# Layer 3's cross attention on turned keys kept in a scratch tensor, two heads at a time on 64 rows

## The reference, cut to what matters

```python
q = layer_norm(x, g_norm) @ Wq                 # 4 x 128 x (16 * 64)
k, v = split(context @ Wkv)                    # 4 x 2048 x (16 * 64) each
k, v = with a null key and value in front of each head's
q = q / |q| * q_scale                          # per head
k = k / |k| * k_scale
attn = softmax(q @ k.T * 8)                    # per head
out = layer_norm((attn @ v) @ Wout, g_out)
```

## Time and profile before

| | us |
|---|---|
| median of 3 runs | 1329.11 (1325.99 to 1330.33) |
| the profiled execution | 1332.39 |
| its span, first to last instruction | 1330.6 |
| TensorE busy | 1129.0 (85%) |
| VectorE busy | 626.6 (47%) |
| ScalarE busy | 425.5 (32%) |
| GpSimd busy | 314.3 (24%) |
| mean granted TensorE clock | 0.894 of full speed |

### The profile page before, as it was taken

How to read it: one execution, slowest core, us unless ns; L and a number is a source line. 1 busy time by engine, 2 the same in 40 slices (tenths; PEclk the granted TensorE clock), 3 DMA queues, 4 the chain that set the end, 5 groups by cost and what they waited for, 6 DMA issues and landing times.

```text
span 1330.6 us, 12990 instructions
## 1 busy us (share of the span) xinstructions
PE 1129.0 (85%) x4750; PEld 648.5 (49%) x4750; DVE 626.6 (47%) x1071; ACT 425.5 (32%) x586; POOL 314.3 (24%) x95
## 2 busy tenths in 40 slices
PE   6996789948799976775877999999999999998558
PEld 4663335727566644452756444454454445444434
DVE  3886762156488863123523434343435344432345
ACT  2663404304265542232116322222222222322011
POOL 0000000000000000000000566546654674565000
PEclk9997799957899986696789999899989998999569
DMA  8100000030000020014000000000000000000100
GB/s 337 79 0 1 0 0 0 1 126 0 1 1 1 1 95 0 0 35 202 1 1 0 16 17 20 16 16 17 20 16 16 16 20 12 20 16 4 69 1 8
DMA packets 21366, 40.15 MB, mean 30 GB/s; under 512 B 2496, under 2 KB 18880, under 8 KB 19648
## 3 DMA queue, kind: packets, MB, share of 16 engines
q1 hardware_dynamic: 21312, 39.41, 8.0%
HBM read 39.14 MB, written 0.26 MB: 30 GB/s over the span
## 4 chain that ended last, share of the span: by engine, by line
PE 77%; DVE 12%; ACT 7%; issue 2%; POOL 1%; DMA 0%; POOLq 0%; DVEq 0%; ACTq 0%
PE PSUM L1918 16%; PE PSUM L1922 16%; PE PSUM L1451 9%; PE PSUM L1512 2%; PE PSUM L1653 2%; PE PSUM L1664 2%; PE PSUM L1483 2%; PE PSUM L1947 1%; PE PSUM L1953 1%; PE PSUM L1460 1%; PE PSUM L2028 1%; DVE ARENA L926 1%; DVE HN L754 1%; PE PSUM L1611 1%; POOL RSTD L366 1%
## 5 line engine op out<-in xcount | busy, mean ns | idle before, releaser
L424 POOL TENSOR_TENSOR ARENA<-ARENA 128x2048 f32<-128x2048 f32 x64 | 288.6, 4510 | 196.5 <-ACT ARENA L684 196.5
L1292 DVE TENSOR_TENSOR ARENA<-PSUM,RK 128x512 f32<-128x512 f32 x256 | 175.6, 691 | 271.7 <-PE PSUM L1918 269.9
L1918 PE MATMUL PSUM<-ARENA,CK 128*128 128x512 f32 x512 | 257.3, 606 | 5.1 <-DVE ARENA L1292 4.3
L1922 PE MATMUL PSUM<-ARENA,CK 128*128 128x512 f32 x512 | 253.4, 598 | 5.8 <-ACT ARENA L706 3.7
L684 ACT ACTIVATE ARENA<-ARENA,CK 128x2048 f32<-128x2048 f32 x64 | 128.1, 2002 | 349.8 <-DVE ARENA L1292 349.8
L1922 PEld LDWEIGHTS PSUM<-ARENA,CK 128*128 128x128 f32 x512 | 97.6, 191 | 131.7 <-issue 113.2
L1918 PEld LDWEIGHTS PSUM<-ARENA,CK 128*128 128x128 f32 x512 | 97.6, 194 | 126.8 <-issue 97.7
L366 POOL TENSOR_TENSOR RSTD<-VE,MHALF 128x4 f32<-128x4 f32 x17 | 17.1, 1008 | 565.3 <-DVE VE L751 565.3
L1451 PE MATMUL PSUM<-WK,CT 128*128 128x512 f32 x256 | 124.1, 607 | 0.0
L454 ACT ACTIVATE SQ<-PSUM 128x512 f32<-128x512 f32 x128 | 76.2, 597 | 67.3 <-PE PSUM L1451 59.5
L773 DVE TENSOR_REDUCE RK<-SQ 128x8 f32<-128x512 f32 x128 | 84.8, 682 | 14.1 <-ACT SQ L454 12.0
(11 more groups left out here) (383 smaller groups left out, 1410.3 us busy)
## 6 DMA issues: line engine op xcount, KB each, us to landing
CT<-in_ctxT SPq DMA_DIRECT2D x4, 1024.0 KB, 10.7
CK<-in_l0f_experts SPq DMA_DIRECT2D x1, 4096.0 KB, 22.9
CK<-in_ctxk SPq DMA_DIRECT2D x1, 4096.0 KB, 12.1
ARENA<-in_l2f_experts SPq DMA_DIRECT2D x2, 2048.0 KB, 8.4
CK<-in_ctxT SPq DMA_DIRECT2D x64, 64.0 KB, 1.8
CK<-in_ctxr SPq DMA_DIRECT2D x64, 64.0 KB, 1.9
ARENA<-in_l2f_experts SPq DMA_DIRECT2D x1, 3072.0 KB, 14.4
WB<-in_wb SPq DMA_DIRECT2D x1, 2798.5 KB, 11.0
```

The source lines that it names most:

```text
L424: nc.gpsimd.tensor_tensor(LS[b % 2], LS[b % 2], PR[:, k % 2, :], ALU.add)\
L1292: ve.tensor_tensor(PR[:, k % 2, c * 512:(c + 1) * 512].rearrange("p (j n) -> p j n", j=4), PSUM[:, c % 2, :].rearrange("p (j n) -> p j n", ...
L1918: mm(bank(c % 2), CTT[:, k, :], qpb[:, b, c * 512:(c + 1) * 512], start=True, stop=True)\
L1922: return mm(bank(4 + c), CKT[:, k, :], PR[:, k % 2, c * 512:(c + 1) * 512], start=first, stop=final, skip_group_check=True)
```

## The change

The keys are now made the other way round: product m multiplies 128 columns of the key matrix (two heads) with 512 context columns, so that it yields turned keys, head width on the partitions. VectorE copies each into one of four staging slots (KST_A in ARENA, KST_B in W8), and SyncE stores it (256 KB) into a scratch tensor `keys` in HBM (`spill_keys`). ScalarE squares the staged copy. The sum over a head's 64 partitions is made by TensorE: four products with `blocks`, a matrix of ones and zeros, each with 32 output columns and each on another column group (`sum_squares_pe`), added up over the 8 pieces of a block of 512 keys in bank 0; VectorE copies the result (`sums_kept_dve`), TensorE transposes it, and VectorE copies that into RK.

In layer 3 the folding is gone. A tile's turned keys (128 partitions x 8 head pairs x 128 keys, 512 KB in pieces of 512 bytes) and its context rows are loaded into four slots. `score` makes half a tile, 8 heads, by 8 products with 64 rows and 128 columns, by turns on the upper and lower 64 rows and into banks 0 and 1. `scale` and `probs` take half a tile each (128x1024). The heads stand in another order (`place`). Half B of the scores uses the same two banks as half A.

```diff
-        QP = ARENA[:, 0:8192]
+        KTB = ARENA[:, 4096:8192].rearrange("p (k q n) -> p k q n", k=4, q=8)
...
+            def spill_keys(staged, m0, n):
+                for m in range(m0, m0 + n):
+                    nc.sync.wait_ge(sem("keys_kept"), SP.due("keys_kept"))
+                    k, p = m // 8, m % 8
+                    sync.dma_start(KEYS[k * P:(k + 1) * P, p * 512:(p + 1) * 512], staged[:, m % 4, :])\
+                        .then_inc(sem("dma_kslot%d" % (m % 4)), 16)
+
+            spill_keys(KST_A, 0, 64)
             nc.sync.wait_ge(sem("x_ready"), SP.due("x_ready", n=3))
             load(CK[:, :, :], d["ctxk"], "dma_ck")
+            spill_keys(KST_B, 64, 64)
...
+            def load_tile(k, keys, rows_):
+                due = SP.due("l3x_gathered", lag=DEEP)
+                if due is not None:
+                    nc.sync.wait_ge(sem("l3x_gathered"), due)
+                sync.dma_start(KTB[:, k, :, :], keys.rearrange("p (q m) -> p q m", q=8)[:, :, k * P:(k + 1) * P])\
+                    .then_inc(sem("dma_kslot%d" % k), 16)
+                sync.dma_start(CKT[:, k, :], rows_).then_inc(sem("dma_kslot%d" % k), 16)
...
-            def key_norms_act(n0, n):
+            def key_norms_act(staged, n0, n):
                 for m in range(n0, n0 + n):
-                    nc.scalar.wait_ge(sem("key_rows"), AC.due("key_rows"))
-                    due = AC.due("key_norm", lag=2)
+                    nc.scalar.wait_ge(sem("keys_kept"), AC.due("keys_kept"))
+                    due = AC.due("key_sums", lag=2)
                     if due is not None:
-                        nc.scalar.wait_ge(sem("key_norm"), due)
-                    act(SQ[:, m % 2, :], bank(5 + 2 * (m % 2)), ACT.Square).then_inc(sem("key_squares"), AC.sends("key_squares"))
+                        nc.scalar.wait_ge(sem("key_sums"), due)
+                    act(SQ[:, m % 2, :], staged[:, m % 4, :], ACT.Square).then_inc(sem("key_squares"), AC.sends("key_squares"))
...
-            qph = QP.rearrange("p (b k h n) -> p b k h n", b=B, k=2, n=P)
-            for b in range(B):
-                for j in range(4):
-                    nc.scalar.wait_ge(sem("l3x_qp"), AC.due("l3x_qp"))
-                    act(qph[:, b, j // 2, j % 2:8:2, :], bank4(j % 2), ACT.Copy).then_inc(sem("l3x_qp_kept"), AC.sends("l3x_qp_kept"))
-
             def probs(k):
-                nc.scalar.wait_ge(sem("l3x_scores_taken"), AC.due("l3x_scores_taken", n=4))
-                act(PR[:, k % 2, :], PR[:, k % 2, :], ACT.Exp, bias=SHIFT).then_inc(sem("l3x_probs"), AC.sends("l3x_probs"))
+                for s in range(2):
+                    nc.scalar.wait_ge(sem("l3x_scores_taken"), AC.due("l3x_scores_taken"))
+                    half = PR[:, k % 2, s * 1024:(s + 1) * 1024]
+                    act(half, half, ACT.Exp, bias=SHIFT).then_inc(sem("l3x_probs"), AC.sends("l3x_probs"))
...
-            def key_norms_dve(n0, n):
+            def sums_turned_dve(n):
+                ve.tensor_copy(RK[:, n * 64:(n + 1) * 64].rearrange("p (c h) -> p c h", c=4),
+                               PSUM[:, 0, P:2 * P].rearrange("p (c w) -> p c w", c=4)[:, :, 0:H])\
+                    .then_inc(sem("key_norm"), DV.sends("key_norm"))
+
+            def sums_kept_dve(n, first):
+
+                nc.vector.wait_ge(sem("key_sums"), DV.due("key_sums", n=8))
+                if not first:
+                    nc.vector.wait_ge(sem("sums_turned"), DV.due("sums_turned"))
+                    sums_turned_dve(n - 1)
+                ve.tensor_copy(NST, PSUM[:, 0, 0:P]).then_inc(sem("sums_kept"), DV.sends("sums_kept"))
+
+            def key_norms_dve(staged, n0, n):
                 for m in range(n0, n0 + n):
-                    nc.vector.wait_ge(sem("key_squares"), DV.due("key_squares"))
-                    ve.tensor_reduce(RK[:, m * 8:(m + 1) * 8], SQ[:, m % 2, :].rearrange("p (h e) -> p h e", e=DH),
-                                     AX.X, ALU.add).then_inc(sem("key_norm"), DV.sends("key_norm"))
+                    nc.vector.wait_ge(sem("key_rows"), DV.due("key_rows"))
+                    if m >= 4:
+                        nc.vector.wait_ge(sem("dma_kslot%d" % (m % 4)), 16 * (m // 4))
+                        nc.vector.wait_ge(sem("key_squares"), m - 3)
+                    ve.tensor_copy(staged[:, m % 4, :], bank(5 + 2 * (m % 2))).then_inc(sem("keys_kept"), DV.sends("keys_kept"))
+                    if m % 8 == 2 and m % 64 != 2:
+                        sums_kept_dve(m // 8 - 1, m % 64 == 10)
+
+            def key_norms_end_dve(n):
+                sums_kept_dve(n, False)
+                nc.vector.wait_ge(sem("sums_turned"), DV.due("sums_turned"))
+                sums_turned_dve(n)
...
             def scale(b, k, t):
-                for c in range(4):
+                for s in range(2):
...
-                    ve.tensor_tensor(PR[:, k % 2, c * 512:(c + 1) * 512].rearrange("p (j n) -> p j n", j=4),
-                                     PSUM[:, c % 2, :].rearrange("p (j n) -> p j n", j=4), each(rk, P), ALU.mult)\
+                    ve.tensor_tensor(PR[:, k % 2, s * 1024:(s + 1) * 1024].rearrange("p (j n) -> p j n", j=8),
+                                     PSUM[:, 0:2, :].rearrange("p r (j n) -> p (r j) n", j=4), each(rk, P), ALU.mult)\
                         .then_inc(sem("l3x_scores_taken"), DV.sends("l3x_scores_taken"))
...
+            def turn_sums_pe():
+
+                nc.tensor.wait_ge(sem("sums_kept"), PE.due("sums_kept"))
+                tp(PSUM[:, 0, P:2 * P], NST, ident).then_inc(sem("sums_turned"), PE.sends("sums_turned"))
+
+            def sum_squares_pe(m):
+
+                n, p = m // 8, m % 8
+                at = 11 - (8 * (p // 4) + p % 4)
+                nc.tensor.wait_ge(sem("key_squares"), m + 1)
+                if p == 0 and n % 8:
+                    nc.tensor.wait_ge(sem("sums_kept"), n)
+                for c in range(4):
+                    last = mm(PSUM[32 * c:32 * c + 32, 0, 0:P], w("blocks")[:, at:at + 32],
+                              SQ[:, m % 2, c * P:(c + 1) * P], start=p == 0, stop=p == 7)
+                last.then_inc(sem("key_sums"), PE.sends("key_sums"))
+                if p == 7 and n % 8:
+                    turn_sums_pe()
+
             def key_norms_pe(n0, n):
                 for m in range(n0, n0 + n):
-                    t, c = m // 2, m % 2
-                    due = PE.due("key_squares", lag=2)
-                    if due is not None:
-                        nc.tensor.wait_ge(sem("key_squares"), due)
-                    mm(bank(5 + 2 * c), CT[:, t * P:(t + 1) * P], WK[:, c * 512:(c + 1) * 512],
-                        start=True, stop=True).then_inc(sem("key_rows"), PE.sends("key_rows"))
+                    k, p = m // 8, m % 8
+                    if m >= 2:
+                        nc.tensor.wait_ge(sem("keys_kept"), m - 1)
+                    mm(bank(5 + 2 * (m % 2)), WK[:, p * P:(p + 1) * P], CT[:, k * 512:(k + 1) * 512],
+                       start=True, stop=True).then_inc(sem("key_rows"), PE.sends("key_rows"))
+                    if m % 64 >= 2:
+                        sum_squares_pe(m - 2)
+
+            def key_norms_end_pe(m):
+                sum_squares_pe(m - 1)
+                sum_squares_pe(m)
+                turn_sums_pe()
...
-            def score(b, k, c):
-                due = PE.due("l3x_scores_taken", lag=2)
+
+            def score(b, k, s):
+                due = PE.due("l3x_scores_taken", lag=1)
                 if due is not None:
                     nc.tensor.wait_ge(sem("l3x_scores_taken"), due)
-                mm(bank(c % 2), CTT[:, k, :], qpb[:, b, c * 512:(c + 1) * 512], start=True, stop=True)\
-                    .then_inc(sem("l3x_scores"), PE.sends("l3x_scores"))
+                for i in range(4):
+                    for r in range(2):
+                        rows_ = slice(DH * r, DH * r + DH)
+                        last = mm(PSUM[:, r, i * P:(i + 1) * P], KTB[rows_, k, 4 * s + i, :],
+                                  QSC[rows_, 4 * s + i, b * P:(b + 1) * P], start=True, stop=True)
+                last.then_inc(sem("l3x_scores"), PE.sends("l3x_scores"))
...
             def tile(b, k, first=False, final=False):
                 b_next = b + 1 if final else b
-                if b_next < B:
-                    nc.tensor.wait_ge(sem("dma_ktile%d" % ((k + 1) % DEEP)), PE.due("dma_ktile%d" % ((k + 1) % DEEP), n=2))
-                    score(b_next, (k + 1) % DEEP, 0)
-                    score(b_next, (k + 1) % DEEP, 1)
-                nc.tensor.wait_ge(sem("l3x_probs"), PE.due("l3x_probs"))
-                if first and b:
-                    nc.tensor.wait_ge(sem("l3x_z_kept"), PE.due("l3x_z_kept"))
-                for c in range(4):
-                    last = gather(k, c, first, final)
-                    if c < 2 and b_next < B:
-                        score(b_next, (k + 1) % DEEP, c + 2)
+                for s in range(2):
```

(47 more changed lines are left out.)

104 lines of the change are left out of this document (45 added, 59 removed).

## The result

The changed kernel takes 1389.55 us (median of 4 runs, 1387.39 to 1392.28) against 1329.72 for the kernel before in the same session: a ratio of 1.045, 95% interval 1.043 to 1.048. The forecast was slower, 1362 us, range 1315 to 1400. The sign and the range held, but the time lies above the likeliest case's own range, 1345 to 1382: the distance from 1329.11 is +60 us where the sum said +33. The profiled execution took 1387.69 us, its span 1385.9, so the two traces differ by 55.3 us, and that is what has to be divided up.

A forecast was written before the change was run, and what follows sets the result against it. TensorE's queue was taken to bound both norm stages and layer 3's loop. Sums +66, waits +25, transposes and ends +8, stores +4, loop -55, folding -15 give +33 us on 1329.11: 1362 us, range 1315 to 1400.

The forecast's parts named there:

- The price of an excursion: TensorE's switch to tiled shape and back costs 0.32 us for column tiles, 0.39 us for two-row tiles, above its steps.
- free changes: Rival: TensorE changes tile shape at no cost where few passes follow; net -55 us, 1274 us; chance 0.16, milder forms included.
- No pairing: Rival: in layer 3's loop 64-row groups don't overlap in full; tile 7.8 us, not 6.0; +115 us, 1475; chance 0.04.
- Sums hidden: Rival: norm stages pay less than 0.52 us a sum because waits and shape changes overlap; -15 us, 1347; chance 0.12.
- The loop: Layer 3's 64 tiles take 6.01 us each in place of 6.87, -55 us.
- Keys late: Rival: in layer 3's loop a tile's load takes over 6 us; +540 us at 14.4 us a load; chance 0.04.
- loop follows VectorE: Rival: in layer 3's loop half A comes 0.3 to 0.6 us later, +10 to +20 us; chance 0.15.
- Folding gone: Ahead of layer 3's loop: folding's 128 passes and 16 copies vanish, so the first gather starts sooner, -15 us.
- The waits for the sums' copy: Norm stages: TensorE waits for VectorE's copy of the sums, 7 x 1.7 and 7 x 1.4 us, within a +25 us term.
- the 3 us for the shifts: Second norm stage: the causal shift holds one copy back by 0.2 us a group, 16 x 0.2, within the +25 us.
- The late first stores: First norm stage: first stores queue behind 4 MB of experts and hold up the fifth key copy and TensorE, +4 us.
- what is added to it there is paid in full: Norm stages and loop: TensorE, busy at full clock 1.00, pays added work in full unless it fills one of few gaps.

The follow-up runs named there:

- run 4: Changed kernel with one full-shape product for the sums in place of four column-tiled ones (norms not those of the reference): 1348.3 us, ratio 1.011 to the kernel before.
- Run 6: run 5 with the sums of four products together in place of two: 1310.3 us, ratio 0.984 to the kernel before.
- run 7: Changed kernel with both score halves of the next tile together ahead of the gathers, for 45 of layer 3's 64 tiles: 1370.9 us, ratio 1.031.
- Run 10: Run 6 with every column-tiled product issued twice in the same excursion (norms not those of the reference): 1329.8 us, ratio 0.999 to the kernel before.
- run 5: Changed kernel with sums of two products together, sums' copy one product earlier, experts' load behind the first stage's stores: 1331.6 us, ratio 0.999 to the kernel before.
- run 8: Changed kernel with all edits of Run 6 and run 7 together: 1291.3 us, ratio 0.969 to the kernel before.
- Run 2: Changed kernel with VectorE's copy of the sums one product earlier: 1363.1 us, ratio 1.023 to the kernel before.
- run 9: Changed kernel with one column tile, weights of ones, in place of four behind each product (norms not those of the reference): 1396.5 us, ratio 1.047.
- run 3: Changed kernel with the 4 MB load of layer 0's experts issued behind the first norm stage's 64 stores: 1386.3 us, ratio 1.037 to the kernel before.

## Why the prediction was right, and what it missed

**The price of an excursion: right.** It was put at 0.32 us for columns and 0.39 for rows, from rows of two column groups of 40 columns and of 8-row tiles. Runs 4 and 6 give 0.33 and 0.33 (0.23 and the next pass's 0.10) for columns, run 7 gives (6.01 - 5.61) = 0.40 for rows. Run 10 shows that it is paid for each change and not for each pass. With it the rival "free changes" is refuted. (By the prediction's own -55 us at no cost and 256 changes that rival turns faster below 0.21 us a change, not 0.26.) The Trainium skill, TensorEngine Tiling (Array Packing), Key Properties, says no more than that a change of mode drains TensorE; these runs agree with a cost at each change, and price it. "No pairing" is refuted by 16 products in 1.10 us. "Sums hidden" is refuted by 1.41 us a product, with the waits beside it.

**The loop: right.** -58.6 us against -55; the 64 tiles of 6.01 us are as worked out, and what is left lies at the four batch changes. "Keys late" is refuted by 3.8 us to landing and by a loop without such a wait, "loop follows VectorE" by 0.46 us of slack where 0.3 was forecast.

**Folding gone: right, -14 us** (-15 forecast). From the last scaled query to the first gather it was 736.7 - 715.8 = 20.9 us, and now, with ScalarE first and TensorE behind it,

```profile
840.80 2.12 ACT L697 ACTIVATE ARENA<-PSUM,CK 128x1024 f32<-128x1024 f32 x2 [0.36 <-PE PSUM L1966]
...
842.97 1.16 PE L1977 MATMUL PSUM<-ARENA 64*128 64x128 f32 x16 [1.34 <-ACT ARENA L697]
845.46 1.16 PE L1977 MATMUL PSUM<-ARENA 64*128 64x128 f32 x16 [1.33 <-DVE ARENA L1338]
848.04 2.08 PE L1977 MATMUL PSUM<-ARENA 64*128 64x128 f32 x16 [1.42 <-DVE ARENA L1338]
850.05 2.93 PE L1982 MATMUL PSUM<-ARENA,CK 128*128 128x512 f32 x3
```

850.05 - 842.92 = 7.1 us, forecast 6.1; the one us more is the third half, which ran at half the clock (2.08 for 1.16). That the rest fits is partly luck: the forecast's own terms, twice 1.16 + 0.33 + 1.22 and then 1.09, add up to 6.5, and a half took 2.5 us (845.46 - 842.97) where they say 2.71.

**The waits for the sums' copy: right in place, a little too large.** 10.4 and 8.3 us, seven waits each of up to 1.6 and 1.2, against 7 x 1.7 and 7 x 1.4; the 3 us for the shifts did not show. 19 in place of 25.

**The late first stores: right in mechanism, too small.** 7.7 us in place of 4. This execution came to its key products 3 us sooner, and the experts' load was issued at 20.32 us and not at 18.75, so that VectorE's key copy went on at 43.55 and not at about 42. Behind the stall stand about 3 us more at a clock of 0.59 (8 us from 42 on). The 3 us at the start come back from the span, so these two nearly cancel; they are no effect of the change, since the first key product starts anywhere from 25.4 to 29.2 us in the runs.

**The step that failed: "what is added to it there is paid in full", at the clock of before.** The sum took every duration of the norm stages at the full clock of the earlier trace rows, 1.00. In the second stage the granted clock went to 0.87, with TensorE busy for 146 of the 155 us, so 0.13 x 155 = some 20 us were missing from the sum. No rival named the clock. Run 6 gives back 13 us beside the 5 of its 16 excursions, about what the clock of 0.90 costs on run 5's 132 us; in run 4 the clock is at 0.99 too. The feed-forward of layer 1, some 13 us behind the stage, ran at 0.50 where before it ran at 0.80.

```profile
490.00:513.00 23.00, 14.87 (x30) 4.92 (x30) 10.09 (x24) 13.34 (x71) 0.00 (x0) 0.80 0.15 62
610.00:633.00 23.00, 20.37 (x30) 5.53 (x30) 6.07 (x11) 13.44 (x70) 0.00 (x0) 0.50 0.13 54
...
536.00:559.00 23.00, 20.16 (x30) 5.31 (x29) 6.29 (x12) 13.45 (x70) 0.00 (x0) 0.50 0.12 52
571.00:594.00 23.00, 20.54 (x30) 5.69 (x30) 5.92 (x10) 13.59 (x71) 0.00 (x0) 0.50 0.15 64
```

The first row is before, the second after: the same 30 matmuls, and from the transposes ahead of them to the products behind them 29.9 us for 25.7, 4 us more. The last two rows are the same matmuls in runs 8 and 4. They ran at 0.50 too, though the second stage had held 0.99 there, and in run 5, whose stage stood at 0.90, they ran at 0.80. So this term does not follow from the stage's low clock, and what decides it is open.

Together: 33 - 6 (waits) + 4 (stores) + 3 (clock behind them) - 3 (start) + 20 (second stage) + 4 (feed-forward) + 1 (folding) - 4 (loop) = +52 of the 55 us in the traces. The other 3 lie between layer 2's experts and layer 3's queries, where no experiment was aimed. None of the missed terms made the sign: without the 27 us put down to the clock the traces would still lie 28 us apart.

**What stays open.** Why the first stage, with the same number of shape changes per product, held 0.98 in the changed kernel (the low stretch there lies behind the stall), while the second fell to 0.87. Run 2 makes this sharper: its first stage has the 64 changes in 123 us with hardly a wait and stands at 0.99, its second has 64 in 144 us and stands at 0.87. In layer 3's loop TensorE changes to row tiles twice in 6.01 us and the clock is 0.98. And in run 9 the first stage fell as well, in run 3 twice, and in run 4 with no column-tiled sum at all. So the number of changes decides within the second stage, and something else decides between the places. The two stages differ in the heads' products between the norms (16 passes on two row groups in layer 0, 8 one after the other in layer 1), but no run tells whether that is it. The Trainium skill, TensorE: Matmul & The Clock Gate, in the section on a second failure mode by PSUM-queue cycling, reports of one kernel that short idles between its groups of matmuls come often enough to make the clock swing between its two levels. The idles that the profile shows as waits are not such ones here, by runs 2 and 4; the time spent in changing shape, during which the profile shows TensorE as busy, may be. That reading is argued and not shown.

## What to carry to other kernels

Count the changes of tile shape and not the tiled passes: here one cost 0.32 to 0.40 us, and tiled work in small portions between full products cost more for its changes than for its work. Collect it: sums in fours and two score halves behind each other, with the early copy of the sums and the experts' load behind the stores, turned a change that was 4.5% slower into one 3% faster, with the same arithmetic. And when work of another kind is put into a stretch that holds the full clock, price a fall of the clock as a rival of its own; 13% of a stage was the largest term that the sum lacked.

## What was unexpected of the hardware

- In the second norm stage a full TensorE queue with many shape changes was granted less than the full clock: 64 changes in 144 us with hardly a wait gave 0.87, 16 in 114 gave 0.99, and no changes with 17 us idle of 130 gave 0.99. It is no general rule: 64 changes in the 123 us of the first stage gave 0.99.
- Within one excursion the column-tiled steps are cheap: 0.19 us for two more steps of four passes side by side, and with one column group in place of four the product and its sum take the same time (1.40 and 1.41 us).
- The 4 MB of experts landed in 12.9 us when issued behind the stores, at 169 us (run 3), and in 22.5 when issued at 20 us, with the loads of the start still under way. The first stores are not what held them up: in the kernel before, without stores, they took 22.9.
